# A four-layer kernel: the second layer's norm inside the first feed-forward, the last layer's first weights and splits made in earlier stages, one mark at a step's end

## The reference

```
for i, (attn, ffn) in enumerate(layers):          # i = 0..3
    xn = (x - mean(x)) / sqrt(var(x) + 1e-5)      # over the 256 features
    x  = x + attn(xn) + ffn(xn)
# layer 0: causal grouped attention, 16 heads   | Hadamard-turned gated ffn, inner size 1024, silu
# layer 1: retention with rotary positions      | norm, then a square product
# layer 2: linear memory and softmax, 16 heads  | product with binarized weights
# layer 3: state-space scan, 32 heads of 64     | mixture of experts, 32 + 32 experts, best 8 of each token
```

## Time and profile before

| | us |
|---|---|
| three executions | 3680.51, 3680.76, 3674.75 |
| their median | 3680.51 |
| the profiled execution, as a whole | 3672.85 |
| its span in the profile | 3671.1 |
| PE busy | 3376.9 (92%) |
| DVE busy | 2423.2 (66%) |
| ACT busy | 1566.8 (43%) |
| POOL busy | 1182.8 (32%) |

### The profile page before, as it was taken

The page is one execution under the profiler, slowest core; times in us unless marked ns, Lnnn a source line. Parts: engine busy times, 40 slices in busy tenths (PEclk is TensorE's granted clock), DMA queues, the critical chain, the costliest instruction groups (busy, mean ns, idle before and its releaser), DMA issues. The chain is left out here.

```text
span 3671.1 us, 65160 instructions
## 1 busy us (share of the span) xinstructions
PE 3376.9 (92%) x21360; PEld 2608.3 (71%) x21360; DVE 2423.2 (66%) x4492; ACT 1566.8 (43%) x2872; POOL 1182.8 (32%) x854
## 2 busy tenths in 40 slices
PE   8999999999979999999986779999779998799997
PEld 6888888887758788888862445555358886488883
DVE  4666666666335666566555778886478887488873
ACT  4555555554324444444432236666233333233332
POOL 4011010200236666666643200000124445344444
PEclk9999999999999999999998879999879999899998
DMA  5000000010001000000001412221144442244331
GB/s 176 4 18 11 7 20 3 26 37 1 0 7 50 18 19 13 19 16 19 17 0 53 154 70 81 81 81 61 61 113 113 111 112 68 58 118 110 108 98 49
DMA packets 134113, 199.98 MB, mean 54 GB/s; under 512 B 23120, under 2 KB 78288, under 8 KB 133968
## 3 DMA queue, kind: packets, MB, share of 16 engines
q1 hardware_dynamic: 127888, 190.55, 16.7%
q0 software_dynamic: 6144, 8.39, 1.4%
HBM read 162.06 MB, written 36.57 MB: 54 GB/s over the span
## 5 line engine op out<-in xcount | busy, mean ns | idle before, releaser
L2137 DVE TENSOR_REDUCE l2h_half<-l2h_s 128x1 f32<-128x512 f32 x512 | 337.2, 685 | 48.0 <-PE l2h_s L2039 45.4
L2124 ACT ACTIVATE l2h_PT<-l2h_s 128x1024 f32<-128x1024 f32 x256 | 248.4, 1023 | 163.5 <-PE l2h_s L2049 163.4
L791 DVE TENSOR_REDUCE l0h_negtop<-l0h_sc 128x1 f32<-128x128 f32 (+7 forms) x256 | 192.7, 753 | 161.9 <-PE l0h_sc L687 161.9
L813 DVE TENSOR_TENSOR l0h_PTL<-l0h_tp,l0h_PTH 128x512 fp32r<-128x512 f32 (+3 forms) x384 | 199.9, 549 | 135.3 <-ACT l0h_PTH L869 135.2
L869 ACT ACTIVATE l0h_PTH<-l0h_tp 128x512 fp32r<-128x512 f32 (+3 forms) x384 | 174.6, 490 | 199.5 <-PE l0h_tp L698 197.7
L2039 PE MATMUL l2h_s<-l2h_K,l2h_Q 128*128 128x512 f32 x512 | 219.1, 466 | 22.7 <-DMA l2h_K<-l_split 20.0
L879 ACT ACTIVATE l0h_probs<-l0h_sc,l0h_negtop 128x128 f32<-128x128 f32 (+7 forms) x256 | 191.1, 746 | 90.0 <-DVE l0h_negtop L791 86.3
L159 POOL TENSOR_TENSOR XN<-XN,n_rstd 128x512 f32<-128x512 f32 x24 | 29.9, 1267 | 566.5 <-DVE n_rstd L140 566.5
L765 POOL TENSOR_TENSOR l0a_wq_lo<-l0a_wq,l0a_wq_hi 128x256 fp32r<-128x256 f32 x15 | 11.1, 741 | 591.2 <-ACT l0a_wq_hi L853 591.2
L698 PE MATMUL l0h_tp<-ident,l0h_probs 128*128 128x128 f32 x1152 | 175.6, 277 | 21.4 <-DVE l0h_PTL L813 21.4
L713 PE MATMUL l0h_cx<-l0h_PTH,l0a_VH 128*128 128x256 f32 (+1 forms) x640 | 183.1, 286 | 0.7 <-DVE l0h_PTL L813 0.7
(11 more groups left out here) (449 smaller groups left out, 9903.9 us busy)
## 6 DMA issues: line engine op xcount, KB each, us to landing
l3p_decb<-l_decays SPq DMA_DIRECT2D x128, 256.0 KB, 4.4
l3p_w<-L_w SPq DMA_DIRECT2D x34, 512.0 KB, 3.7
l2h_Q<-l_split SPq DMA_DIRECT2D x64, 256.0 KB
l2h_K<-l_split SPq DMA_DIRECT2D x64, 256.0 KB
l3p_prow<-l_decays SPq DMA_DIRECT2D x128, 128.0 KB, 3.1
l_split<-l2q_hi SPq DMA_DIRECT2D x16, 512.0 KB, 3.6
l_split<-l2q_lo SPq DMA_DIRECT2D x16, 512.0 KB, 3.8
l3p_wgu<-L_ffn_w_gate_up SPq DMA_DIRECT2D x32, 256.0 KB, 4.8
```

The source lines that it names most:

```text
L791: dve.reduce_max(negtop[:, i % 4:i % 4 + 1], sc[s % 2][:, 0:(t + 1) * P], AX_X, negate=True).then_inc(top_ready, 1)
L813: dve.tensor_tensor(PTL[part], tp[n % 2][:, 0:m * P].rearrange("p (m n) -> p m n", m=m), PTH[part].bitcast(F32), ALU.subtract).then_inc(pt ...
L2124: act.activation(PT[:, b, kb, :], s2[kb % 2][:, :], ACT.Exp, scale=L2_SCALE).then_inc(exped, 1)
L2137: dve.reduce_max(half[:, b, t, z:z + 1], bank(slot_of(i))[:, :], AX_X).then_inc(s1_read, 1)
```

## The change

1. **Norm of layer 1 inside `l0_ffn`.** In each of the three blocks j of the loop, the norm of block j - 1 is made between the instructions of block j: PE's mean products before slice 2 and variance products before slice 5, in the two `turn` banks; DVE's centring before slice 3's `hidden`; ACT's square before slice 4's silu and its square root before slice 7's silu; DVE's reciprocal before `add(j)`; POOL's scaling behind its 8 low parts; the high part (ACT) behind the slices and the low part (DVE) behind `add(j)`. The norm of the last block stands behind the loop. `norm_stage` for n1 and `split_stage` are gone; XH and XL of layer 0 are kept for layer 1.
2. **Layer 3's first weights, constants and splits earlier.** The weight tiles, the four constants and XH now live for the whole layer. The front stage loads pair 0's weights and the constants and makes XH, w_hi (ACT, between its copies of `rowsN` and `bcol`) and XNL, w_lo (POOL). For the second sequence XH and XNL are made in `l3_output` of the first (ACT, DVE); its pair 0's weights are those that the last step of the first sequence had already split, a result that before was made and thrown away. `split_in_place` is gone, and so is the first `split_weights` in `l3_pairs`.
3. **In the first step of `l3_pairs`** `table(0)` stands behind the projections of x and b instead of ahead of them, and `turn_rows(0)` behind the sums of the states.
4. **One mark at a step's end.** `mark(h + 1, 0)`, before in the middle of step z = 0, stands at that step's end, behind the updates of the states. `mark(h + 1, 1)` stays.

The core of the diff:

```
+                def mean_of(j):
+                    pe.wait_ge(added, (j + 1) * DC + 1)
+                    pe.wait_ge(centred, j + 1)
+                    for c in range(DC):
+                        mm = pe.matmul(mean[:, :], k.avg[:, :], k.XT[:, c, tok(j)], start=(c == 0), stop=(c == DC - 1))
+                    mm.then_inc(mean_ready, 1)
+
+                def var_of(j):
+                    pe.wait_ge(squared, j + 1)
+                    pe.wait_ge(std_ready, j + 1)
+                    for c in range(DC):
+                        mm = pe.matmul(var[:, :], k.avg[:, :], sq[:, c, :], start=(c == 0), stop=(c == DC - 1))
+                    mm.then_inc(var_ready, 1)
...
                 def block_of(j):
                     for f in range(L0_FC):
+                        if not isinstance(j, int):
+                            if f == 2:
+                                mean_of(j - 1)
+                            elif f == 5:
+                                var_of(j - 1)
...
                 with pe.Fori(1, NJ) as j:
                     block_of(j)
+                mean_of(NJ - 1)
+                var_of(NJ - 1)
...
+                def square(j):
+                    act.wait_ge(centred, j + 2)
+                    act.wait_ge(var_ready, j + 1)
+                    act.activation(sq[:, :, :], k.XN[:, :, tok(j)], ACT.Square).then_inc(squared, 1)
+
+                def root(j):
+                    act.wait_ge(var_ready, j + 2)
+                    act.wait_ge(rstd_ready, j + 1)
+                    act.activation(std[:, :], var[:, :], ACT.Sqrt, bias=k.eps[:, 0:1]).then_inc(std_ready, 1)
+
+                def high_x(j):
+                    for c in range(DC):
+                        act.wait_ge(scaled, DC * j + c + 2)
+                        act.activation(k.XH[:, c, tok(j)], k.XN[:, c, tok(j)], ACT.Copy).then_inc(xhi_ready, 1)
...
+                        if not isinstance(j, int):
+                            if f == 4:
+                                square(j - 1)
+                            elif f == 7:
+                                root(j - 1)
...
                     keep_high(j, L0_FC - 1)
+                    if not isinstance(j, int):
+                        high_x(j - 1)
...
+                def scale(j):
+                    pool.wait_ge(rstd_ready, j + 2)
+                    for c in range(DC):
+                        pool.tensor_tensor(k.XN[:, c, tok(j)], k.XN[:, c, tok(j)], rstd[:, :], ALU.mult).then_inc(scaled, 1)
...
+                block_of(0)
+                with pool.Fori(1, NJ) as j:
+                    block_of(j)
+                    scale(j - 1)
+                scale(NJ - 1)
...
+                def centre(j):
+                    dve.wait_ge(mean_ready, j + 1)
+                    for c in range(DC):
+                        op = dve.tensor_tensor(k.XN[:, c, tok(j)], k.XT[:, c, tok(j)], mean[:, :], ALU.subtract)
+                    op.then_inc(centred, 1)
+
+                def invert(j):
+                    dve.wait_ge(std_ready, j + 2)
+                    dve.wait_ge(scaled, DC * j + 1)
+                    dve.reciprocal(rstd[:, :], std[:, :]).then_inc(rstd_ready, 1)
+
+                def low_x(j):
+                    for c in range(DC):
+                        dve.wait_ge(xhi_ready, DC * j + c + 1)
+                        dve.tensor_tensor(k.XL[:, c, tok(j)], k.XN[:, c, tok(j)], k.XH[:, c, tok(j)].bitcast(F32), ALU.subtract)
...
                     for f in range(L0_FC):
+                        if f == 3:
+                            centre(j - 1)
                         hidden(j, f)
+                    invert(j - 1)
                     add(j)
+                    low_x(j - 1)
+                centre(NJ - 1)
+                invert(NJ - 1)
+                low_x(NJ - 1)
...
+                sp.dma_start(ssm.w4[:, :, :, :], a["L3_w4"][0]).then_inc(w4_loaded, 16)
+                sp.dma_start(ssm.eye4[:, :], a["c_eye4"]).then_inc(consts_loaded, 16)
+                sp.dma_start(ssm.blk[:, :], a["c_l3_block"]).then_inc(consts_loaded, 16)
+                sp.dma_start(moe.slots[:, :], a["c_moe_slots"].to_broadcast([P, P])).then_inc(consts_loaded, 16)
+                sp.dma_start(moe.spare[:, :], a["c_moe_spare"]).then_inc(consts_loaded, 16)
...
+                for n, (c, tok) in enumerate(split_parts()):
+                    pool.wait_ge(xhi_ready, n + 1)
+                    pool.wait_ge(turned, turns)
+                    pool.tensor_tensor(k.XNL[:, c, tok], k.XN[:, c, tok], ssm.XH[:, c, tok].bitcast(F32), ALU.subtract)
+                pool.wait_ge(whi_ready, 1)
+                pool.tensor_tensor(ssm.w_lo[:, :, :, :], ssm.w4[:, :, :, :], ssm.w_hi[:, :, :, :].bitcast(F32), ALU.subtract)
...
+                for c, tok in split_parts():
+                    act.activation(ssm.XH[:, c, tok], k.XN[:, c, tok], ACT.Copy).then_inc(xhi_ready, 1)
+                act.wait_ge(w4_loaded, 16)
+                act.activation(ssm.w_hi[:, :, :, :], ssm.w4[:, :, :, :], ACT.Copy).then_inc(whi_ready, 1)
...
                 def step(h, z):
                     project(h, z, (0, 1))
+                    if is_first(h, z):
+                        table(0)
                     if z == NZ - 1:
                         gate_up(h)
                     project(h, z, (2, 3))
                     if not is_first(h, z):
                         outputs(*before(h, z))
-                    if z == 0:
+                    if z == 0 and not is_first(h, z):
                         turn_rows(h)
-                    else:
+                    elif z:
                         down(h)
                     scores(h, z)
                     if z == NZ - 1 and more(h):
                         table(h + 1)
                     state_sums(h, z)
-
-                table(0)
+                    if is_first(h, z):
+                        turn_rows(h)
+
                 steps(pe, step)
                 outputs(L3_PAIRS - 1, NZ - 1)
...
-                split_weights(0)
+                pool.sem_inc(wlo_ready, 1)
...
-                    if more(h):
-                        mark(h + 1, z)
+                    if z and more(h):
+                        mark(h + 1, 1)
...
+                    if z == 0 and more(h):
+                        mark(h + 1, 0)
...
+                if b + 1 < B:
+                    for c, tok in split_parts():
+                        act.activation(ssm.XH[:, c, tok], NEXT[:, c, tok], ACT.Copy).then_inc(xhi_ready, 1)
...
+                if b + 1 < B:
+                    for n, (c, tok) in enumerate(split_parts()):
+                        dve.wait_ge(xhi_ready, n + 1)
+                        dve.tensor_tensor(NEXT_LOW[:, c, tok], NEXT[:, c, tok], ssm.XH[:, c, tok].bitcast(F32), ALU.subtract)
```

141 lines of the change are left out of this document (57 added, 84 removed).

## The result

The changed kernel took 3642.24 us (median of 3647.14, 3642.89, 3639.11 and 3641.59), the kernel before, on the same chip, 3677.63 (median of four): a ratio of 0.9899, 95% interval 0.9881 to 0.9918, so 35.4 us faster. The forecast was 3643 us and 34.2 us of gain. The sum was right within what can be measured, and part of that is luck, because two terms in it were wrong and their errors are hidden: the first step of the pairs costs more than was forecast, and the moved mark is worth more, against losses that were not seen.

A forecast was written before the change was run, and what follows sets the result against it. PE was taken to bound feed-forward and pairs, chains of other engines and DMAs the stretches between. Gains 7.5 + 10.7 + 13.9 + 2.1 = 34.2 us, from 3677.2 to 3643 us; own range 3634 to 3652, 8 in 10 3632 to 3657.

The forecast's parts named there:

- The norm in the feed-forward: Layer 0's feed-forward: 18.5 us gained behind the last block, 11.0 paid on PE in three turns, net 7.5 us.
- The margin of ACT and POOL: Last feed-forward block: slice 7's low part, delayed by ACT's table loads, still reaches PE in time by 0.4 us.
- that of the reciprocal: Last feed-forward block: DVE's reciprocal is done 0.5 us ahead of the addition at 1055.67.
- Rival 1: Feed-forward: each ACT table switch holds 1.38 us longer, late silu, PE waits 7 us in all; 3650 us; chance 8%.
- First sequence: Layer 3's entry: 15.5 us gained before PE's first projection, 0.6 charged for the table, 4.2 in front stage; net 10.7.
- The front stage: Layer 3's front stage: POOL's subtractions hold DVE's chain, costing 4.2 us, ends 0 and 7.4.
- Second sequence: Layer 3's second entry: 14.5 us gained up to PE's first projection, 0.6 charged for the table, net 13.9.
- the moved table: First step of layer 3's pairs: the table, now behind 12 products, was charged 0.6 us in each sequence.
- rival 2: Layer 3's pair entries: other waits (decay rows, gathered rows, code) replace those removed; 13 us less gain, 3656 us; chance 15%.
- The mark: Layer 3's pairs, step z = 0: removed wait for `l3p_btok` gives 0.07 us in 30 steps, 2.1 us (0 to 5.7).
- Rival 3: Layer 3's pairs: the mark at step end meets POOL's two-operand work, DVE becomes the bound; slower, up to 3721 us; chance 3%.
- The signs of being wrong: A pair above 24.0 us, a PE wait above 2 us in the pairs' first step, or a feed-forward turn above 39.5.

## Why the prediction was right, point by point

- **The norm in the feed-forward: right.** 15.3 us behind the last block (15.2), 10.4 for three turns (11.0), net 8.0 (7.5). The margin of ACT and POOL was 0.2 to 0.3 us (0.4), that of the reciprocal 0.58 (0.5). Rival 1 did not come: the silu follows the second load, and in the run with two more loads each cost its 1.28 and nothing behind it. Here the Trainium skill's 2.66 per switch (ScalarE: Activation LUTs, "What ACT_TABLE_LOAD costs") does not hold; the measurement decides.
- **First sequence: size right, by two errors.** From `key` to the first projection 0.3 us, not 1.6: PE is released while the memset runs (2692.09 to 2693.04), so the increment behind it in the list doesn't wait for it. That gave 1.3 more. But the first step cost 3.7 us instead of 0.6, because I looked at the marks, scans and table and not far enough along the chain: table, row numbers, gather, rows. With PE's list started early, that chain is late at the step's end: 1.9 us with what stands around the wait of 1.70. The early start alone would not have done it: the gather began 7.5 us behind PE's start and the rows were wanted at 12.2, so with the old landing of 3.1 us they would have been in time by 1.5 (estimate). It was the landing of 6.3. The DMA engines were at 0.96 of their time meanwhile, with the loads that the stage issues at its entry; that these loads are the cause is argued, no run has moved them. The masked b is 0.2 late. The table itself is 0.5, and the products take 1.2 more, 8.3 us for the 24 instead of 7.1, of which 1.0 is the clock: PE's first 12 products run at the lower level (granted clock 0.50 from 2692.1 to 2697.4), 0.63 us each, where before it was 7. The front stage lost 3.7 (4.2 forecast), and its cause is shown. Here the trace agrees with the Trainium skill (SBUF — State Buffer, "Who interferes with whom"), by which a DVE instruction with two SBUF inputs contends with a GpSimd instruction that reads SBUF; that a plain copy is also held, 1.55 instead of 0.60 us, was not forecast. Net: 16.9 - 3.8 - 3.7 = 9.4, forecast 10.7.
- **Second sequence: 16.1 - 4.8 = 11.4, forecast 13.9.** The 16.1 were forecast as 14.5; here too PE starts with the memset (3158.72 and 3158.66) and not behind it. Same step, same cause: the 0.6 for the moved table should have been 4.8 (1.93 for the rows, 0.85 for the masked b, 0.5 for the table, the rest with the clock, which is at the lower level again behind the wait, 0.63 us a product). This is rival 2's mechanism, decay rows and gathered rows both, with 2.5 us of 13.9 lost instead of 5.
- **The mark: the term that was mis-sized.** It was put at 2.1, with "0.07 us in each of 30 steps" read from a wait of 0.19 in one pair. Moved alone it gives 4.6 in the profile; in the changed kernel its return costs 12.1 there and about 10 in the timed runs. What the step lacked is that the pairs have two orders, and 0.013 us of distance parts them. Parts 2 and 3 shift sequence 1 from 0.24 to 0.29 and into the late order, which by itself costs 10 us; the mark's new place hides just that. In the changed kernel the pairs show only 0.8 and 1.3 us of gain, 2.0 in all, and the 2.1 forecast looked right. That is luck: the mark gives over 4, and the loss of the next point takes half of it back.
- **Something is still paid in the pairs.** A pair of sequence 2 takes 24.02 us in the changed kernel and 23.93 in the kernel before with the mark moved, both without a wait for the masked b; the 0.09 builds up in the four projections, most of it in those of one of the two steps, whose operands lie elsewhere in SBUF now. With XL and two other tiles moved once more (the run with the parts made earlier), sequence 1 is at 23.89 instead of 23.98. Whether the addresses are the cause wasn't tried.
- **Rival 3** (the mark at the end makes DVE the bound) did not come: no pair above 24.1. But it named the right danger, DVE held by GpSimd's two operands in this step, and had it on the wrong side: the mark in the *middle* is what makes that expensive.
- **The signs of being wrong.** Of the three, one came by a hair: pairs of sequence 2 take 24.02 us (the first full one 24.09), above the 24.0 named. The waits of the first steps were 1.70 us, and 0.85 and 1.93, each below the 2 us named, but in sequence 2 together above it; the turns were 38.1, as forecast. The signs pointed at the two places where terms were wrong, while the total did not.

## What to carry to other kernels

When work is taken off the critical path at a stage's entry, follow each chain that used to hide behind it to its last link, DMAs included; the first wait found is seldom the only one. Where two engines exclude each other, a shift of some hundredths of a microsecond can turn their order in every turn of a loop: look at the distance, put work with slack between the held instruction and its reader, and time each part of a change also alone and taken back, since one part may be paying for another. Work for GpSimd on two SBUF operands was free here only where DVE stood anyway.

## What the runs showed of the hardware that was not expected

- DVE's update against GpSimd's gather: passes in 0.35 us up to 0.246 us behind its start, held 2.2 us from 0.259 on, in 330 steps of eleven profiles without an exception. A memset of DVE ahead of it moves the update (by 0.13 and 0.27 us) and the edge with it; the second instruction of such a pair then takes 0.23 instead of 0.35. By the end of the DVE instruction ahead of both, the edge lies between 0.211 and 0.224 us in all 420 steps.
- A gather of GpSimd that starts 0.10 to 0.65 us behind the start of a DVE scan with two SBUF operands took 2.23 to 1.68 us (five profiles); the same gather took 1.30 where no scan ran when it began.
- The rows of a gather landed mostly 2.7 to 2.9 us behind its start, and 5.6 to 8.0 in the first steps of the kernels that start PE early, with the DMA engines at 0.83 to 1.00 of their time.
- A memset of GpSimd ahead of a gather delays it by 0.03 us only.
- A load of ACT's table costs 1.28 us, also when four stand within 7 us.
- A wait of 1.8 us of PE, once in each turn of 41 us, was followed in one of three turns by 6.8 us at a granted clock of 0.50.
